# Moving gate, up and hidden-transpose jobs across the pass boundary, and small steps off GpSimd, in a pipelined attention and FP4 feed-forward kernel

## The reference

```python
xn = _layernorm(x)
x = x + attn(xn) + ffn(xn)
# attn: 16 heads of 8, 4 key/value heads, causal softmax, rotary q and k
q = rope(xn @ Wqa @ Wqb); k, v = split(xn @ Wkva @ Wkvb)
attn = softmax(mask(q k^T * scale)) v @ Wout + bout
# ffn: every operand is quantised blockwise to FP4 values and back
lin(x, w) = einsum(fp4(x), fp4(w))       # fp4: blocks of 16, scale = max|x|/6
ffn = lin(silu(lin(xn, w_gate)) * lin(xn, w_up), w_down)     # 352 hidden features
```

## Time and profile before

| | us |
|---|---|
| median of 3 runs (lowest, highest) | 807.89 (806.34, 809.37) |
| the profiled execution, its time | 808.11 |
| its span in the profile | 806.0 |
| TensorE busy | 718.5 (89%) |
| VectorE busy | 641.2 (80%) |
| GpSimd busy | 612.4 (76%) |
| ScalarE busy | 535.1 (66%) |
| granted TensorE clock, mean | 0.98 |

### The profile page before, as it was taken

One profiled execution on the slowest core, in us unless ns is written; L12 is line 12 of the kernel. 1 busy time (PEld: TensorE's weight loads), 2 busy tenths in 40 slices (PEclk: granted clock), 3 DMA queues, 4 the chain that ended last, 5 costly groups with the idle time before them and its releaser, 6 DMA issues.

```text
span 806.0 us, 18255 instructions
## 1 busy us (share of the span) xinstructions
PE 718.5 (89%) x6354; PEld 444.2 (55%) x6445; DVE 641.2 (80%) x1378; ACT 535.1 (66%) x1154; POOL 612.4 (76%) x708
## 2 busy tenths in 40 slices
PE   2366889999999999999999999999999999999773
PEld 1233555665656565656656565656566565656243
DVE  5569788989888988889898889888898988788110
ACT  2212677777686867777777868677777777575850
POOL 4534597878799797978787897979787888756560
PEclk9998899999999999999999999999999999999995
DMA  4423233243343334343434333343324333330111
GB/s 111 114 67 96 63 93 95 89 116 96 103 111 103 88 114 106 112 100 91 115 97 107 102 110 87 113 106 116 96 90 118 94 95 111 88 92 29 56 55 28
DMA packets 85589, 76.04 MB, mean 94 GB/s; under 512 B 28946, under 2 KB 67314, under 8 KB 85498
## 3 DMA queue, kind: packets, MB, share of 16 engines
q1 hardware_dynamic: 85498, 74.87, 34.3%
HBM read 40.73 MB, written 27.53 MB: 85 GB/s over the span
## 4 chain that ended last, share of the span: by engine, by line
PE 35%; POOL 32%; ACT 14%; issue 6%; DVE 6%; DMA 3%; SPq 2%; another core or an unknown queue 1%; POOLq 0%; DVEq 0%; ACTq 0%
POOL P L535 9%; PE pv_ps L1111 8%; PE exp_ps L1090 6%; POOL h L545 5%; ACT P L912 5%; PE max_ps L1075 5%; POOL h L548 5%; POOL h L551 4%; PE misc_ps L1135 3%; PE misc_ps L1143 3%; DVE neg_max L718 3%; PE max_ps L1076 3%; PE misc_ps L1160 3%; ACT h_mag L1019 3%; POOL q_split L626 2%
## 5 line engine op out<-in xcount | busy, mean ns | idle before, releaser
L718 DVE TENSOR_REDUCE neg_max<-max_ps 128x1 f32<-128x512 f32 (+3 forms) x768 | 429.1, 591 | 88.3 <-PE max_ps L1076 86.6
L912 ACT ACTIVATE P<-exp_ps 128x512 f32<-128x512 f32 x512 | 294.9, 599 | 167.0 <-remote 100.4
L1075 PE MATMUL max_ps<-K,Q 128*128 128x384 bf16 (+2 forms) x768 | 199.2, 278 | 23.4 <-DMA Kd<-K 11.2
L1090 PE MATMUL exp_ps<-Q,K 128*128 128x128 bf16 (+3 forms) x933 | 209.9, 293 | 10.8 <-ACT P L912 6.7
L1076 PE MATMUL max_ps<-Kd,Q 128*128 128x128 bf16 x1024 | 191.4, 221 | 1.4 <-DVE neg_max L718 1.3
L535 POOL TENSOR_SCALAR_AFFINE_SELECT P<-P 128x512 f32<-128x512 f32 x256 | 161.9, 667 | 26.8 <-ACT P L915 26.8
L1111 PE MATMUL pv_ps<-P,V 128*32 128x512 f32 (+3 forms) x2048 | 163.9, 438 | 1.9 <-POOL P L535 0.8
L1075 PEld LDWEIGHTS max_ps<-K,Q 128*128 128x128 bf16 x768 | 75.9, 100 | 92.1 <-DVE neg_max L718 47.1
L1076 PEld LDWEIGHTS max_ps<-Kd,Q 128*128 128x128 bf16 x1024 | 98.6, 100 | 45.6 <-issue 23.2
L1090 PEld LDWEIGHTS exp_ps<-Q,K 128*128 128x128 bf16 x1024 | 79.6, 98 | 48.6 <-ACT P L912 27.0
L566 POOL TENSOR_TENSOR h<-gate_sb,up_half 128x352 f32<-128x352 f32 x64 | 59.7, 932 | 56.8 <-DVE gate_sb L731 56.6
(11 more groups left out here) (109 smaller groups left out, 977.5 us busy)
## 6 DMA issues: line engine op xcount, KB each, us to landing
Q<-q_scr SPq DMA_DIRECT2D x64, 224.0 KB
o_scr<-oT SPq DMA_DIRECT2D x32, 256.0 KB, 2.5
q_scr<-q_split SPq DMA_DIRECT2D x16, 384.0 KB, 2.6
Kd<-K SPq DMA_DIRECT2D x64, 96.0 KB
x_in<-x SPq DMA_DIRECT2D x16, 256.0 KB, 4.6
q_scr<-q_split SPq DMA_DIRECT2D x16, 256.0 KB, 2.9
x_res<-x SPq DMA_DIRECT2D x16, 256.0 KB, 5.5
o_raw<-o_scr SPq DMA_DIRECT2D x32, 128.0 KB
```

Source lines behind the costliest of these rows:

```text
L718: nc.vector.tensor_reduce(neg_max[:, pr // 4, heads[0]:heads[0] + len(heads), pr % 4, i], max_ps[r % 3][:, 0:len(heads) * n].rearrange("p ...
L912: nc.scalar.activation(P[g % 2][:, hh + r % 2, col:col + 512], ps[:, :], ACT.Exp, scale=SCALE).then_inc(exp_done, 1)
L1075: nc.tensor.matmul(ps[:, col:col + d], Qt, Kt[:, half, g, 0:d], start=True, stop=True)
L1090: last = nc.tensor.matmul(exp_ps[n % 2][:, col:col + width], K[par][:, half, pr // 2, kb * 128:(kb + 1) * 128], Q[par][:, pr, kb * 128:S], ...
```

## The change

1. MISC: gate0 and up0 move from slot 0 of the pass (sequence T+1) to slot 7 of the pass before it (sequence T+2). The transposes hqT0, hqT1, hqT2 move from slot 7 of their pass to slots 0, 0 and 4 of the next one. h gets a third buffer for that.
2. GpSimd: `hidden` of tile 0 moves to the end of the pass; scaling h (L542) moves ahead of the three steps on the FP4 input. The copies of v (L610), the first, second and fourth of the small steps of `statistics`, and the addition of the bias (L648) leave it.
3. VectorE: two copies of v straight from PSUM into V (three buffers) in place of one copy into a stage; it adds EPS (behind `reduces(3, 4)`) and forms `shift` with one scalar_tensor_tensor, just ahead of `reduces(5, 0)`; `gated` of tile 0 moves to slot 7 and `hidden_max` of tile 0 from slot 1 to slot 0.
4. The bias becomes one more row of w_down, against a row of ones in hqT; the residual x_res is loaded at the top of the pass that uses it.
5. TensorE's wait for the prepared weights stands before slot 7 of pass -2 and not behind that pass.

```diff
 MISC = [
-    [[("gate0", 0, 1), ("up0", 1, 1)], [("xnT", 1, 2)], []],
+    [[("hqT0", 0, -1)], [("xnT", 1, 2)], [("hqT1", 0, -1)]],
...
-    [[("gate3", 0, 1), ("up3", 1, 1)], [], []],
+    [[("gate3", 0, 1), ("up3", 1, 1)], [], [("hqT2", 1, -1)]],
...
-    [[("hqT0", 1, 0)], [("hqT1", 0, 0)], [("hqT2", 1, 0)]],
+    [[("gate0", 0, 2), ("up0", 1, 2)], [], []],
 ]
+def ahead(f):
+    return 2 if f == 0 else 1
...
-                if T.has(0):
-                    T.wait(sp, x_bias_done, 1, 0, 0)
-                    sp.dma_start(x_res[:, :, :], x[T.batch(0)].rearrange("(c p) e -> p c e", p=128)).then_inc(x_res_loaded, 16)
+                if T.has(-1):
+                    T.prev().misc_wait(sp, misc_read, "out1")
+                    sp.dma_start(x_res[:, :, :], x[T.batch(-1)].rearrange("(c p) e -> p c e", p=128)).then_inc(x_res_loaded, 16)
...
-            def statistics(T):
+            def deviation(T):
...
-                T.wait(pool, mv_done, NT, 3, NT)
-                nc.gpsimd.tensor_scalar(var_eps[:, :], bn_mv[:, :, 1], EPS, None, ALU.add).then_inc(var_done, 1)
-                nc.gpsimd.tensor_scalar(neg_mean[:, :], bn_mv[:, :, 0], -1.0, None, ALU.mult).then_inc(var_done, 1)
-                T.wait(pool, var_done, 2, 3, 2)
+                T.wait(pool, var_done, 1, 3, 1)
                 nc.gpsimd.tensor_tensor(rstd[:, :], var_eps[:, :], half_neg[:, :], ALU.pow).then_inc(rstd_done, 1)
-                T.wait(pool, rstd_done, 2, 3, 1)
-                nc.gpsimd.tensor_tensor(shift[:, :], neg_mean[:, :], rstd[:, :], ALU.mult).then_inc(rstd_done, 1)
...
                 split_rest(T, 0, 1)
-                hidden(T, 0)
+                if T.has(0):
+                    quantize(T, 0, 0, *hs)
...
-                    for s in range(2):
-                        nc.gpsimd.tensor_copy(V[T.par(1)][:, :, s::2, D * s:D * s + D],
-                                              v_stage[:, :, :].rearrange("p c (g d) -> p c g d", g=KVH)[:, :, s::2, :]).then_inc(v_ready, 1)
...
-                    nc.gpsimd.tensor_tensor(x_bias[:, :, :], x_res[:, :, :],
-                                            bout_sb[:, :].unsqueeze(1).to_broadcast([128, NT, E]), ALU.add).then_inc(x_bias_done, 1)
...
+                hidden(T, 0)
...
-                gated(T, 0)
+                hidden_max(T, 0)
...
-                reduces(3, 4, 5)
+                reduces(3, 4)
+                if T.has(3):
+                    T.wait(dve, mv_done, NT, 3, NT)
+                    T.wait(dve, rstd_done, 2, 2, 1)
+                    nc.vector.tensor_scalar(var_eps[:, :], bn_mv[:, :, 1], EPS, None, ALU.add).then_inc(var_done, 1)
+                reduces(3, 5)
...
-                    nc.vector.tensor_copy(v_stage[:, :, :], misc_ps[1][:, 0:128].rearrange("p (c n) -> p c n", c=NT)).then_inc(misc_read[1], 1)
+                    for odd in range(2):
+                        nc.vector.tensor_copy(V[T.third(2)][:, :, odd::2, D * odd:D * odd + D],
+                                              misc_ps[1][:, 0:128].rearrange("p (c g d) -> p c g d", c=NT, g=KVH)[:, :, odd::2, :]
+                                              ).then_inc(v_ready if odd == 0 else misc_read[1], 1)
...
+                if T.has(3):
+                    T.wait(dve, rstd_done, 2, 3, 1)
+                    nc.vector.scalar_tensor_tensor(shift[:, :], bn_mv[:, :, 0], -1.0, rstd[:, :],
+                                                   ALU.mult, ALU.mult).then_inc(rstd_done, 1)
                 reduces(5, 0)
                 normalize(T)
...
-                reduces(7, 3, 4, 5)
+                reduces(7, 3)
+                gated(T, 0)
+                reduces(7, 4, 5)
...
-                        for k, (_, cn) in enumerate(FC):
+                        for k, cn in enumerate((FC[0][1], FC[1][1], FC[2][1] + 1)):
```

More of the change, by code:

```diff
@@ L90, in batch, with third @@
         return self.t0 + off
+    def third(self, off):
+        return (self.t0 + off) % 3
     def wait(self, eng, sem, per, off, k):
@@ L191, in build @@
         Kd = sb("Kd", [128, 2, KVH, S], BF16)
-        V = [sb(f"V{i}", [128, NT, KVH, 32]) for i in range(2)]
+        V = [sb(f"V{i}", [128, NT, KVH, 32]) for i in range(3)]
         P = [sb(f"P{i}", [128, GH, P_WIDTH]) for i in range(2)]
@@ L216, in build @@
         up_half = [sb(f"up_half{i}", [128, F]) for i in range(2)]
-        h = [sb(f"h{i}", [128, NT * F]) for i in range(2)]
+        h = [sb(f"h{i}", [128, NT * F]) for i in range(3)]
         h_max = sb("h_max", [128, NT * F // BLOCK])
@@ L318, in spread, with iterate @@
             return ap.unsqueeze(2).to_broadcast([ap.shape[0], ap.shape[1], BLOCK])
-        def iterate(eng, iteration, then=None):
+        def iterate(eng, iteration):
             for t in range(FIRST_T, LAST_T + 1):
                 iteration(Step(t))
-                if t == FIRST_T + 1 and then:
-                    then()
         @block.sync
@@ L515, in _ @@
             nc.gpsimd.memset(half_neg[:, :], -0.5).then_inc(consts_set, 1)
-            for i in range(2):
+            for i in range(3):
                 nc.gpsimd.memset(V[i][:, :, :, :], 0.0).then_inc(pool_const, 1)
@@ L520, in _ @@
             nc.gpsimd.memset(m_split[:, :, 64:128], 0.0).then_inc(pool_const, 1)
-            pool.wait_ge(pool_const, 5)
-            for i in range(2):
+            pool.wait_ge(pool_const, 6)
+            for i in range(3):
                 nc.gpsimd.memset(V[i][:, :, 0::2, 2 * D:2 * D + 1], 1.0).then_inc(pool_const, 1)
@@ L560, in hidden @@
             def hidden(T, f):
-                if not T.has(1):
+                off = ahead(f)
+                if not T.has(off):
                     return
@@ L722, in gated @@
             def gated(T, f):
-                if not T.has(1):
+                off = ahead(f)
+                if not T.has(off):
                     return
-                T.wait(dve, th_done, NT, 1, f + 1)
+                T.wait(dve, th_done, NT, off, f + 1)
                 T.misc_wait(dve, misc_filled, f"gate{f}")
-                T.wait(dve, h_made, NT, 1, f - 1)
+                T.wait(dve, h_made, NT, off, f - 1)
                 nc.vector.scalar_tensor_tensor(gate_sb[f % 2][:, :], th[f % 2][:, :], 1.0, misc_ps[0][:, 0:F],
@@ L765, in output @@
                 if n == 0:
-                    T.wait(dve, x_bias_done, 1, -1, 1)
+                    T.wait(dve, x_res_loaded, 16, -1, 16)
                     T.wait(dve, stored, 32, -1, 0)
@@ L831, in iteration @@
                     T.wait(dve, x_loaded, 16, 3, 16)
-                    T.wait(dve, var_done, 2, 2, 2)
                     for c in range(NT):
@@ L1104, in weighted_sums @@
                     if g == 0:
-                        T.wait(pe, v_ready, 2, off, 2)
+                        T.wait(pe, v_ready, 1, off, 1)
+                        T.prev().prev().misc_wait(pe, misc_read, "v")
                 else:
@@ L1110, in weighted_sums @@
                     for j in range(GH):
-                        last = nc.tensor.matmul(pv_ps[32 * j:32 * j + 32, kb * 128:S], V[T.par(off)][:, kb, g, :],
+                        last = nc.tensor.matmul(pv_ps[32 * j:32 * j + 32, kb * 128:S], V[T.third(off)][:, kb, g, :],
                                                 P[g % 2][:, j, P_COL[kb]:P_COL[kb] + width],
@@ L1133, in misc_job @@
                     f = int(job[-1])
-                    T.prev().misc_wait(pe, misc_read, "xqT")
-                    last = nc.tensor.matmul(ps[:, 0:F], xqT[T.par(1)][:, tok[f]], wguT[:, int(job[0] == "u"), :], start=True, stop=True)
+                    (T if f == 0 else T.prev()).misc_wait(pe, misc_read, "xqT")
+                    last = nc.tensor.matmul(ps[:, 0:F], xqT[T.par(off)][:, tok[f]], wguT[:, int(job[0] == "u"), :], start=True, stop=True)
                 elif job == "xnT":
@@ L1157, in misc_job @@
                     c0, cn = FC[int(job[-1])]
-                    T.wait(pe, h_quant, 3, 0, 3)
+                    T.wait(pe, h_quant, 3, -1, 3)
                     for c in range(NT):
-                        last = nc.tensor.transpose(ps[0:cn, tok[c]], h[T.par(0)][:, c * F + c0:c * F + c0 + cn], ident[:, :])
+                        last = nc.tensor.transpose(ps[0:cn, tok[c]], h[T.third(-1)][:, c * F + c0:c * F + c0 + cn], ident[:, :])
                 elif job.startswith("mrow"):
@@ L1165, in misc_job @@
                 elif job in ("out0", "out1"):
+                    T.misc_wait(pe, misc_read, "hqT1")
+                    T.misc_wait(pe, misc_read, "hqT2")
                     T.wait(pe, o_normed, 1, -1, 1)
@@ L1178, in iteration @@
                         transpose_weights()
+                    if slot == 7 and T.t0 == FIRST_T + 1:
+                        weights_stored()
                     max_tile(T, slot, 0)
```

46 lines of the change are left out of this document (18 added, 28 removed).

## The result

The changed kernel takes 832.7 us (median of 4, 827.2 to 839.3), the kernel before 808.0 beside it: 1.031 times as long, 95% interval 1.023 to 1.039. The profiled execution took 831.8 us with a span of 829.7, so 23.7 us of span were added where 5.2 were forecast. The direction and the place were right; the time lies above the range. Executions over 1.5% above a kernel's fastest count as its slower state and stay out of the ratios: five of e3's ten (806.6 to 808.0 us), and one of 1481.8 us of the kernel before, run beside e1 to e4.

What follows compares the result with a forecast made beforehand. TensorE, held up by waits for GpSimd and VectorE, was taken as the nearest bound. Terms +23.0 (onT), -10.1, -1.9, -2.2 and -3.6 summed to +5.2 us, giving a median of 813.1 us, range 794 to 819.

Steps and rivals of the forecast that it cites:

- boundary 0/1: Between passes 0 and 1, where TensorE stands 1.51 us at hqT0: about -1.9 us.
- passes 13, 14 and the tail: Boundaries 13/14 and 14/15, and hqT copies leaving ScalarE's last slot: -2.2 us together, bounds 0 to -4.
- start: gate0/up0 run during DMA waits, -1.9, and x_mag lies behind L542, -1.7: -3.6 us, bounds -1 to -5.5.
- The lock on onT: Slot 5: onT waits for GpSimd's running addition (L545), about 2.7 us instead of 1.3, ending 0.56 after it.
- Rival A: Slot 5: onT slips in before GpSimd's addition, costing only shift, +1.8 us; about 792 us; chance 0.22 with near cases.
- The tipping point: Slot 5: onT goes first if GpSimd starts L545 by less than 0.7 us earlier, or VectorE is that much faster.
- Price: 1.92 us a pass, bounds 1.3 and 2.2: Slot 5: onT's later end delays the next pass equally; paid in passes 1 to 12, +23.0 us.
- hidden in the same wait: End of slot 3: VectorE's four-column EPS step, bound 0 to 0.22 us, is covered by VectorE's wait for TensorE.
- Slots 7, 0 and 1: One transpose and two TensorE stands leave: 0.84 us a pass saved, kept 0.4 to 1.2; 12 passes, -10.1 us.
- rival C: VectorE bounds slots 7 to 1, gain there only 0.4 us: about 818 us, or 822; chance 0.12.
- The stand at hqT0: TensorE's wait for GpSimd's L551 goes, as hqT0 is issued over 5 us later: 0.26 to 0.45 us saved.
- the one at xnT: TensorE's stand at xnT goes, as bank 1 is free: 0.14 to 0.33 us saved.

Runs made afterwards that it cites:

- e3: Changed kernel with onT formed by a tensor_reduce that only copies o_raw (one SBUF input, multiplication left out): 798.9 us, ratio 0.989.
- e1: Changed kernel with all four small layernorm statistics steps back on GpSimd: 800.75 us, 0.992 of the kernel before.
- e4: Changed kernel with a useless memset of 1024 columns on GpSimd ahead of the first big addition: 804.6 us, ratio 0.998.
- e12: Changed kernel with GpSimd's first big addition waiting for onT, and x_mag moved to slot 7: 797.9 us, ratio 0.988.
- e5: Kernel before with the moves alone; GpSimd keeps the four statistics steps, the bias and the v copies: 800.3 us, ratio 0.991.
- e9: Changed kernel with only EPS on VectorE; negated mean, rstd and shift on GpSimd: 840.9 us, ratio 1.040.
- e10: Changed kernel with only shift on VectorE; EPS and rstd on GpSimd, negated mean gone: 841.7 us, ratio 1.042.
- e6: Changed kernel with 24 idle matmuls of 128 columns on TensorE ahead of its wait for onT: 822.75 us, ratio 1.021.
- e11: e1 with x_mag moved from ScalarE's slot 0 to the end of the slot 7 before it: 797.7 us, ratio 0.988.
- e2: Kernel before with only the EPS addition and the shift step moved to VectorE: 838.3 us, ratio 1.040.

## Why the prediction was right and where it failed

By span, forecast and measured:

| term | forecast | measured |
|---|---|---|
| a regular pass, x12 | +1.08 x 12 = +12.9 | +1.31 x 12 = +15.7 |
| passes 3, 8, 6 and 9, beyond that | 0 | +12.6 |
| boundary 0/1 | -1.9 | -0.1 |
| passes 13, 14 and the tail | -2.2 | +1.3 |
| start | -3.6 | -5.8 |
| sum | +5.2 | +23.7 |

**The lock on onT: right.** onT at 2.82 us (about 2.7 foretold), its end 0.56 behind the addition's, the addition back at 2.85, x_scale at 0.17. The price was 1.92 us a pass and measured 1.79 in slots 4 and 5, hqT2 in slot 4 included. The addition came 1.02 us earlier after k_split, where I had 0.86 to 0.95. e3, e4 and e12 show the mechanism, each with another edit. Rival A is out, though its place was the right one to name: e1 and e5 are rival A, with onT first by 0.54 us, and give 800 to 801 us where A had 792. The tipping point that I gave, 0.7 us, is the margin of the kernel before; with the moves made it is 0.54 (e1), and 0.55 less in e9 tips it.

**The step that failed: "Price: 1.92 us a pass, bounds 1.3 and 2.2".** It priced the stand and not what the stand does to TensorE. Behind it most of what is left of slot 5 runs at 1.2 instead of 2.4 GHz in some passes, 1.6 us each: in four of them here, some 6.4 us of the 12.6, and in up to eleven of twelve in e9 and e10. e6 shows it: busy through the same stand, TensorE keeps its clock in every pass. No row of the kernel before had such a stand in a steady pass, but the slow clock at the start was in the rows.

**The second: EPS, "hidden in the same wait".** I put 0 to 0.22 us on a four-column step. By the lock that I had just read out of the trace its price was that of whatever GpSimd runs beside it. It was caught behind q_split (0.92 us), and then shift and onT each waited for an addition, 2.11 and 2.93 us: passes 3 and 8 are 4.6 and 4.7 us longer, 1.6 of each by the clock, so some 6.1 us of the 12.6 are of this. I never looked at which of EPS and q_split starts first, with 0.28 us between them, nor where shift lands once VectorE is 1 us late.

**Slots 7, 0 and 1: 0.46 us a pass, not 0.84,** all of it in slot 7; within the bounds of 0.4 to 1.2, and near the 0.4 of rival C. Over twelve passes that is 4.6 us of the miss. The stand at hqT0 went, as foretold. In slot 0 TensorE has 0.20 us less to do (5.30 to 5.10 busy), but a stand of 0.39 us for ScalarE took the place of the one at xnT. ScalarE is not late: the second P ends 2.37 us after the slot's first matmul (449.58), as before. TensorE is early, with hqT0 (0.60 us) where gate0 and up0 (1.35) were. What ScalarE does there bounded the gain. I had named VectorE as the engine near its limit there and not looked at ScalarE; with it relieved (e11) VectorE is next, 0.14 us on.

**Start and end.** The start gave more than its bound of 5.5; the 1.7 us that I had put there on x_mag had no row behind it, and no run tries it. The boundary 0/1 gave nothing: TensorE stands 1.42 us for VectorE at the end of slot 7 of pass 0, and slot 0 of pass 1 takes 6.17 us, before 5.48. Of the end I had said that copies leave ScalarE's last slot; they land in slots 0 and 4, in passes 15 and 16 too, where TensorE has no max tiles and ScalarE's exponentials set the length: from slot 0 of pass 15 to the end are 61.0 us, before 59.5. That this is ScalarE is read from the slots' lengths (slot 0 4.63 us, before 3.94; slot 4 4.14, before 3.70) and was not tried by itself.

**Not settled:** why the clock falls in one pass and not in the next after the same stand. Longer stands go with more falls: after 1.52 to 1.54 us the clock fell in 2 of 10 passes, after 2.15 in both (the changed kernel), after 1.87 to 2.01 in 29 of 36 (e2, e9, e10). Nor is it settled why EPS is caught in no to three of the passes 1 to 12. The spread of the changed kernel's runs (827 to 839 us) would fit both; only profiled executions tell, one for each kernel.

## What to carry to other kernels

Where an instruction of VectorE with two inputs in SBUF (or with one, as EPS here) meets one of GpSimd that reads SBUF, the quantity to watch is whether it or GpSimd's instruction starts first, with the margin in time, and not the load of either engine. A lighter GpSimd can cost up to a long instruction's full length, and a wait that pins the order can be the cheapest edit there is (here 1.36 us of GpSimd's waiting bought 1.7 us of a regular pass). Price a stand of TensorE twice, once with the clock kept and once with what follows at half the clock. A small step is priced by what runs beside it, not by its columns, and it has a margin of its own to be read.

## What the runs showed of the hardware

- A reduction with one SBUF input (0.67 us) isn't held up by GpSimd's addition, nor is the two-input multiplication by a memset (0.67). But the two-input multiplication is held up by the addition (2.82), and a tensor_scalar of four columns with one SBUF input is held up (0.92 us instead of 0.16 beside q_split).
- With onT waiting for one addition, the next one of GpSimd is recorded longer (3.19 us, not 2.85) and onT ends first: the waiting instruction gets in before GpSimd's next.
- A stand of 1.52 us at the end of a stretch in which TensorE was busy 2.41 of 4.07 us was followed, 1.2 us on, by a granted clock of 0.59 over 4.13 us; 1.53 us and 2.42 of 4.08 in the next pass were followed by 1.00. Longer stands (1.87 to 2.01 us) were followed by a fall in 29 of 36 passes. Idle matmuls through the stand kept the clock at 1.00 in every pass from 1 to 12.
